# An integer feed-forward with features on the partitions, and a mixture's routing done earlier, on one Trainium2 core

## The reference

```python
probs = jax.nn.softmax(flat @ gate_W.T, axis=-1)
top_v, top_i = jax.lax.top_k(probs, 2)
routed = sum over e of gates[:, e] * (silu(flat @ w1_e[e]) * (flat @ w3_e[e])) @ w2_e[e]
```

```python
def act_qdq(x):                       # 16 bits, one scale for the tensor
    scale = jnp.maximum(jnp.max(jnp.abs(x)) / 32767.0, 1e-12)
    return jnp.clip(jnp.round(x / scale), -32768.0, 32767.0) * scale
x = act_qdq(x)
up = act_qdq(x @ lpbq_dequant(w_up).T)
gate = act_qdq(x @ lpbq_dequant(w_gate).T)
sig = fixed_qdq_u16(jax.nn.sigmoid(gate))
gate = act_qdq(gate * sig)
o = act_qdq(gate * up)
return o @ lpbq_dequant(w_down).T
```

## Time and profile before

| | us |
|---|---|
| median of three runs | 2027.38 |
| the profiled execution, its own time | 2024.79 |
| its span, first to last instruction | 2023.0 |
| mixture up to its loop (first product of the lists at) | 777.0 |
| integer feed-forward, gate (1413.54 to 1469.11) | 55.6 |
| up (1469.11 to 1525.38) | 56.3 |
| second product and its scales (1525.38 to 1561.26) | 35.9 |
| down (1561.26 to 1619.17) | 57.9 |

### The profile page before, as it was taken

One profiled execution on the slowest core, in us unless ns is written; L12 is line 12 of the kernel. 1 busy time (PEld: TensorE's weight loads), 2 busy tenths in 40 slices (PEclk: granted clock), 3 DMA queues, 4 the chain that ended last, 5 costly groups with the idle time before them and its releaser, 6 DMA issues. The chain is left out here.

```text
span 2023.0 us, 38916 instructions
## 1 busy us (share of the span) xinstructions
PE 1860.2 (92%) x13727; PEld 1509.8 (75%) x13728; DVE 1258.4 (62%) x4605; ACT 833.9 (41%) x2271; POOL 278.8 (14%) x514
## 2 busy tenths in 40 slices
PE   8899998999998999999999998997992989999987
PEld 6567766667766998999999998776551867778754
DVE  7768875877786271111111145677788539999988
ACT  3433335565554111111111111775487424445468
POOL 2001112000001051000000044432000320001022
PEclk9999998999999899999999999899995989999999
DMA  6211112111110913222222012110100031111100
GB/s 230 89 55 44 51 47 79 43 70 56 43 43 8 303 55 107 88 86 86 88 86 86 26 53 58 55 44 9 58 1 0 0 107 35 36 38 37 27 11 33
DMA packets 106724, 124.98 MB, mean 62 GB/s; under 512 B 36160, under 2 KB 85832, under 8 KB 104776
## 3 DMA queue, kind: packets, MB, share of 16 engines
q1 hardware_dynamic: 95704, 107.64, 16.1%
q0 software_dynamic: 3072, 8.39, 1.3%
q10 hardware_dynamic: 7792, 6.95, 1.0%
HBM read 86.39 MB, written 36.63 MB: 61 GB/s over the span
## 5 line engine op out<-in xcount | busy, mean ns | idle before, releaser
L1804 DVE TENSOR_TENSOR me_h<-me_sg,me_ps_u 128x512 f32<-128x512 f32 x106 | 72.8, 687 | 273.2 <-PE me_ps_u L1615 273.1
L1756 ACT ACTIVATE me_sg<-me_ps_g 128x512 f32<-128x512 f32 x106 | 63.3, 597 | 363.7 <-PE me_ps_g L1615 363.7
L1276 ACT ACTIVATE ca_e<-ca_scored,ca_neg_max 128x256 f32<-128x256 f32 x256 | 127.2, 499 | 110.4 <-DVE ca_neg_max L1335 110.4
L1615 PE MATMUL me_ps_g<-me_x_turned,me_w 128*128 128x128 f32 x1184 | 145.8, 277 | 1.9 <-issue 1.9
L1615 PEld LDWEIGHTS me_ps_g<-me_x_turned,me_w 128*128 128x128 f32 x1184 | 142.2, 194 | 4.2 <-issue 2.3
L1615 PE MATMUL me_ps_u<-me_x_turned,me_w 128*128 128x128 f32 x1184 | 144.3, 275 | 0.0
L1623 PE MATMUL me_ps_y<-me_w,me_h 128*128 128x256 f32 x592 | 140.0, 380 | 0.0
L1615 PEld LDWEIGHTS me_ps_u<-me_x_turned,me_w 128*128 128x128 f32 x1184 | 138.2, 192 | 0.0
L2995 ACT ACTIVATE sc_y_all<-ss_v 128x16 f32<-128x16 f32 x256 | 60.9, 238 | 148.3 <-DVE ss_v L3060 146.8
L1623 PEld LDWEIGHTS me_ps_y<-me_w,me_h 128*128 128x128 f32 x592 | 106.9, 191 | 11.3
L1335 DVE CUSTOM_DVE_ANT_0 ca_scored<-ca_main,ca_mask_add 128x256 f32<-128x256 f32 x256 | 93.0, 420 | 25.9 <-PE ca_main L1219 25.9
(11 more groups left out here) (465 smaller groups left out, 4374.3 us busy)
## 6 DMA issues: line engine op xcount, KB each, us to landing
me_w<-in_L_ffn_w_e SPq DMA_DIRECT2D x24, 1024.0 KB, 8.1
ca_k_list<-kv_out SPq DMA_DIRECT2D x28, 256.0 KB, 2.3
ca_v_list<-kv_out SPq DMA_DIRECT2D x28, 256.0 KB, 2.3
sk_gb<-scan_g_band SPq DMA_DIRECT2D x14, 512.0 KB, 3.6
moe_x_list<-me_zeros SPq DMA_DIRECT2D x1, 5248.0 KB, 21.2
me_x_tile<-moe_x_list SPq DMA_DIRECT2D x38, 128.0 KB, 2.0
moe_y_list<-me_y ACTq DMA_DIRECT2D x37, 128.0 KB, 1.7
ca_kT<-ca_k_list SPq DMA_DIRECT2D x4, 1024.0 KB, 4.8
```

The costliest lines, as they stand in the source:

```text
L1276: nc.scalar.activation(e[:, g % 3, e_, it, :], scored[:, g % 2, e_, it, :], ACT.Exp, scale=-1.0, bias=neg_max[:, g % 2, n:n + 1], accum_ou ...
L1615: last = nc.tensor.matmul(ps[:, j * P:(j + 1) * P], w[:, n, kt, f:f + P], x[:, kt, :], start=(kt == 0), stop=(kt == KD - 1))
L1756: nc.scalar.activation(sg[:, c, :], ps_g[c][:, :], ACT.Silu).then_inc(done, 1)
L1804: nc.vector.tensor_tensor(h[:, c, :, :].rearrange("p j n -> p (j n)"), sg[:, c, :], ps_u[c][:, :], ALU.mult).then_inc(done[c], 1)
```

## The change

In the integer feed-forward the gate and up products are computed turned: the weights are stationary, 128 features of them, and 1024 tokens are streamed. The result has features on the partitions, in 12 units (6 blocks of features by 2 halves of the tokens) in place of 16 tiles of 768. So the down product can take h as it is, and `turn_h` and `copy_h` go. The elementwise steps work on 1024 columns in place of 768. The ring of integers has three buffers of 1024 in place of four of 768. x is rounded, turned and copied in pairs of tiles. The 16 groups of the next weights are spread over 12 units by `parts_beside`. In the mixture the choice of experts comes before tile 0, the counts inside it, and the placing, cut in two, in tile 1; POOL waits after each three tiles of the scatter until these have landed.

```diff
@@ stage_moe
+    GROUP = 3
+            def count_rows(at):
+                if at != 4:
+                    return
+                pe.wait_ge(both_ready, 1)
+                nc.tensor.matmul(ps_r[:, 0:TILES * E], before[:, :], flat, start=True, stop=True)
...
-                    early(t)
-                if t == 2:
-                    pe.wait_ge(both_ready, 1)
...
+                    early(t, count_rows if t == 0 else nothing)
@@ DVE
             shift_logits()
-            early(0)
             choose_experts()
-            early(1)
+            early(0, behind=scan_counts)
+            early(1, place_experts, place_tokens)
             early(2)
-            scan_counts()
             early(3)
-            place_tokens()
@@ POOL
             for t in range(TILES):
+                if t % GROUP == 0 and t > 0:
+                    pool.wait_ge(scattered, 16 * TOP * t)
@@ int_gate_first, now int_turned
+    WIDE = 1024
+    UNITS = 2 * FT
+    PAIRS = TILES // 2
-    RING = 4
+    RING = 3
-        gi, ui = st.sb("gi", [P, RING, FF], I16), st.sb("ui", [P, RING, FF], I16)
+        gi, ui = st.sb("gi", [P, RING, WIDE], I16), st.sb("ui", [P, RING, WIDE], I16)
+        def piece(w, n):
+            c, f = divmod(n, FT)
+            return w[:, f, WIDE * c:WIDE * (c + 1)]
+        def parts_beside(n):
+            return range(n * len(parts) // UNITS, (n + 1) * len(parts) // UNITS)
@@ PE
+            def half(w, n, side):
+                c, f = divmod(n, FT)
+                t = 8 * c + 4 * side
                 for kt in range(KD):
-                        last = nc.tensor.matmul(ps[t % 2][:, lo:hi], xT[:, t, kt * P:(kt + 1) * P], wT[:, w, kt, lo:hi],
+                    last = nc.tensor.matmul(ps[n % 2][:, side * 512:(side + 1) * 512], wT[:, w, kt, f * P:(f + 1) * P],
+                                            xT[:, t:t + 4, kt * P:(kt + 1) * P], start=(kt == 0), stop=(kt == KD - 1))
-            for t in range(TILES):
-                if t + 1 < TILES:
-                    turn_x(t + 1)
-                gate_product(t)
+            for n in range(2, UNITS):
+                if n + 2 < PAIRS:
+                    turn_x(n + 2)
+                gate_half(n, 0)
+                gate_half(n, 1)
-            for t in range(TILES):
-                up_product(t)
-                turn_next(t)
+            for n in range(UNITS):
+                up_product(n)
+                for g in parts_beside(n):
+                    turn_next(g)
-            schedule(pe, TILES, ((2, turn_h), (3, down)))
+            schedule(pe, TILES, ((2, down),))
@@ ACT
+            for n in range(UNITS - 1):
+                if n + 4 < PAIRS:
+                    copy_x(n + 4)
+                keep_gate(n)
+                if n in (6, 8, 10):
+                    ternary((n - 6) // 2)
-            for t in range(TILES):
-                if t + 1 < TILES:
-                    integers(t + 1)
-                sigmoid(t)
-                keep_up(t)
-                if t >= 1:
-                    copy_next(t - 1)
+            for n in range(UNITS):
+                if n + 1 < UNITS:
+                    integers(n + 1)
+                sigmoid(n)
+                keep_up(n)
+                if n >= 1:
+                    for g in parts_beside(n - 1):
+                        copy_next(g)
-            schedule(act, TILES, ((0, scale_h), (2, copy_h)))
+            schedule(act, TILES, ((0, scale_h),))
```

More of the change, by code:

```diff
@@ L1931, in place_tokens @@
                 link(nc.vector.tensor_copy(table[:, :], first[0:1, :]))
+            def place_tokens():
+                first = starts[:, 4, :]
                 link(nc.vector.tensor_tensor(place[:, 0, :, :], scan[:, 4, :, :], sums[:, :, :], ALU.subtract))
@@ L2443, in gate_product, with turn_x @@
[L2443 to L2451, removed]
-                else:
-                    pe.wait_ge(up_kept, t - 1)
-                multiply(1, t, up_mm)
+            def turn_x(p):
+                pe.wait_ge(x_ready, p + 1)
+                if p >= 2:
+                    pe.wait_ge(xT_ready, p - 1)
+                for m in range(2):
+                    for kt in range(KD):
+                        lo = m * D + kt * P
+                        last = nc.tensor.transpose(ps_x[p % 2][:, lo:lo + P], xi[:, p % 2, m, kt * P:(kt + 1) * P],
+                                                   core.ident[:, :])
+                last.then_inc(x_ps, 1)
@@ L2470, in _ @@
             turn_x(0)
-            for t in range(TILES):
-                if t + 1 < TILES:
-                    turn_x(t + 1)
-                gate_product(t)
-            pe.wait_ge(ident_ready, 1)
-            for t in range(TILES):
-                up_product(t)
-                turn_next(t)
-            pe.wait_ge(product, 2 * TILES - 1)
-            for _ in range(WARM):
[L2481 to L2492, removed]
+            turn_x(1)
+            gate_half(0, 0)
+            turn_x(2)
+            gate_half(1, 0)
+            turn_x(3)
+            gate_half(0, 1)
+            gate_half(1, 1)
+            for n in range(2, UNITS):
[3 more added lines that the diff above has]
+                gate_half(n, 1)
+            pe.wait_ge(ident_ready, 1)
+            for n in range(UNITS):
+                up_product(n)
+                for g in parts_beside(n):
+                    turn_next(g)
+            pe.wait_ge(product, 2 * UNITS - 1)
+            for _ in range(WARM):
+                nc.tensor.matmul(ps_x[1][:, 0:P], core.ident[:, :], core.ident[:, :], start=True, stop=True)
             def down(t, par):
@@ L2573, in _ @@
+            for g in parts_beside(UNITS - 1):
+                copy_next(g)
             act.wait_ge(all_scaled, 1)
-            for t in range(TILES):
-                gate_integers(t)
-                up_integers(t)
+            for n in range(UNITS):
+                gate_integers(n)
+                up_integers(n)
             def scale_h(t, par):
                 if later(t):
-                    act.wait_ge(h_ready, t - 1)
-                nc.scalar.activation(a[:, par, :], gate[:, t, :], ACT.Identity, scale=scal[:, 13:14],
+                    act.wait_ge(hT_ready, t - 1)
+                nc.scalar.activation(a[:, par, :, :], out[:, :, t, :], ACT.Identity, scale=scal[:, 13:14],
```

269 lines of the change are left out of this document (127 added, 142 removed).

## The result

The changed kernel takes 2068.24 us (median of four runs, 2067.25 to 2069.34) where the kernel before takes 2026.47 (median of four): a ratio of 1.0208, 95% interval 1.0193 to 1.0224. It is slower by 42 us. The forecast was 2062.5 with 2042 to 2071.

The account below looks back on a forecast made before the run. PE was taken to bound gate and down, VectorE up and the second product. Mixture -2.5, gate +3.4, up +48.6, second product -0.3, down -12.1 sum to +37.1 on 2024.79: 2061.9, taken as 2062.5 us, range 2042 to 2071.

Parts of the forecast that it names:

- both loops: Up: ring of three delays ScalarE's integers; PE's next-weight group waits for a copy behind the same unit's keep; +48.3 us.
- First product: Up: 13.4 us pass from the last gate unit until VectorE's first product, instead of 10.7.
- Short turns: Up: turns held only by the ring of three buffers take 5.23 us where 4.12 was due.
- The long loop with the clock kept: Up: chain through ScalarE, PE and VectorE where a group needs its own unit's copy; 10.0 us, 11.8 with fallen clock.
- Rival (a): Up: widening wins, neither loop bites, up costs -0.1, total 2013.2 us; turns under 4.9 us make it faster; chance 0.10.
- Rival (b): Up: only the ring bites, copies don't hold PE; up +9.6, total 2023.4 us, no change; chance 0.04.
- Rival (c): Up: both loops bite but TensorE's clock is kept, 6 x 1.8 us less, total 2051; chance 0.14.
- A restart: Up: TensorE's clock falls in each of six long idles, costing 1.7 us more and 0.1 on the small group.
- Gate: Gate part: +3.4 us (0 to +6); PE waits 1.8 at units 2 to 5, 0.9 for the fourth pair.
- Second product: Second product: VectorE's 29.6 us becomes 28.6, fill +0.4, last maximum +0.3, ring of three has slack; -0.3.
- Down: Down part: turnings of h go, -12.1 us; +1.7 if the clock fell in the idle before it.
- Mixture: Mixture: slots ready near 694 instead of 721, scatter done at worst 765; gain 1.7 to 3.3 us, taken 2.5.

Follow-up runs that it names:

- the run with the idle filled: Changed kernel, with unread identity products on TensorE in up ahead of eight next-weight groups' copy waits: 2053.65 us, ratio 1.0146.
- the run with both edits: Changed kernel, in up ScalarE copies next weights ahead of its integers, and the integer ring has four buffers: 2015.65 us, ratio 0.9953.
- the run with copies first: Changed kernel, in up ScalarE copies the previous unit's next-weight groups ahead of integers, sigmoid and kept product: 2022.63 us, ratio 0.9996.
- all repairs together: Changed kernel, up copies ahead of integers, four ring buffers, gate keep ahead of the pair copy, 20 warming products for 14: 2006.46 us, ratio 0.9912.
- the run of the mixture's part alone: Kernel before, with only the change's mixture part (earlier choice, counts and placing, scatter in groups of three tiles): 2020.00 us, ratio 0.9976.
- a ring of four: Changed kernel, gate integers in up get four buffers instead of three, copies left in place: 2034.58 us, ratio 1.0053.
- one group a unit: Changed kernel, next-weight groups spread one to each of the first eleven units, the last five behind the twelfth: 2024.37 us, ratio 1.0002.

## Why the prediction was right, step by step

**Up: right, both loops.** First product: 13.4 forecast, 13.5 measured. Short turns: 5.23 forecast, 5.21 measured. Which turns are long: units 2, 3, 5, 6, 8 and 9, six, as forecast. The long loop with the clock kept: 10.0 forecast, 9.8 in the run with the idle filled. Taken apart on the chip: without the copy wait 52.3 us, without the ring wait 59.5, without either 42.5, against 93.6 with both. Rival (a), that widening wins, is what the run with both edits shows once the two waits are out (2015.65 against the rival's 2013.2); but its own condition, turns under 4.9 us, did not hold in the changed kernel. Rival (b), only the ring bites, is the run with copies first (2022.63 against 2023.4; the terms as written add up to 2023.2). Rival (c), clock kept, is the run with the idle filled (2053.65 against 2051).

**Up: one size too small.** A restart was taken from single restarts in the earlier trace rows as 1.7 + 0.1; the six products behind an idle took 5.71, 6.44, 5.92, 4.96, 5.39 and 6.49, a mean of 2.2 over 3.65, and the filled run gives 2.27 a turn where 1.8 was booked: +2.8 over six. With the clock kept the six turns came out 0.4 shorter than booked (58.9 in the filled run, against 6 x 10.0 - 0.7 = 59.3); the 0.7 for narrower copies is in it, since the last three long turns there are 0.11, 0.33 and 0.32 shorter than the first three. Together 2.4, about this part's miss of 2.3. "Were only the first to pay, the sum would be 8.5 less" counts five restarts at 1.7; at the booked 1.8 it is 9.0.

**Gate: right mechanism, two terms wrong.** Four waits of 1.69 (forecast 1.8) and 0.69 for the fourth pair (0.9). But the 5.1 us of DVE waits in the earlier trace rows were booked as a gain nearly whole. The timeline of before has 1.25 and 0.56 of them ahead of its first gate product, a start that was priced separately (+1.2); only 3.3 could go, 1.2 less than the 4.5 booked. And the slow start was booked as becoming shorter, while it became longer. Before, the first eight records took 4.58 where the next eight took 2.75, 1.8 too much. After, two rows of four records took 3.78 and 2.46 and the four turn records between them 1.06, where 1.88, 1.88 and 0.60 are the times at full clock, 2.9 too much. So the miss of 2.4 us is 1.2 for the waits, 1.1 for the longer slow start and 0.7 for the gain that was booked for it, less 0.6 by which the new waits came out under the forecast.

**Second product: right** (-0.3).

**Down: -10.1 for -12.1.** The "+1.7 if the clock fell" was named and costed at nothing, because idles of 1.1 cost nothing before. In the profiled execution the idle was 1.85 and the clock did fall: the records took 1.68 more than in the runs where it held. With the clock kept the part takes 46.1 (all repairs together), -11.8 for -12.1. No run shows why it fell here, so this term is luck either way: with the same 14 warming products it held in five of seven profiled executions, over idles of up to 2.26.

**Mixture: right**, and at the good end of its range. Slots at 692.5 (forecast 694), no late h, 0.5 for the first listed tile, the last scatter issue at 747.4 (at worst 765), and the clock kept behind the 1.9 us, as in the other two executions with this part of the change. The 1.0 us that the execution was ahead before the mixture's first product is not the change's: that work is the same, and the run of the mixture's part alone has that product at 670.9, as before.

The misses of up, gate and down have one sign, +6.7 us, and most of it is time at half clock that was booked too low. The mixture and the start took 1.8 back, which was not foreseen for the start and is luck. The range held what was left, 5.4 over the sum (with 0.5 behind the block), because its upper bound took in restarts that cost half clock for a whole unit.

## What to carry to other kernels

When work of N pieces is spread anew over M steps, ask of each piece not how many there are in a step but how old the release is that it needs. Here the same 16 groups, the same copies and the same queues cost 40 us when a copy was needed in its own turn and at most 1.2 when it was a turn older. A wait that closes a loop through three in-order queues costs its whole length in every turn, while each engine looks half idle, and two such loops don't add: cutting either one gains most (41 or 34 us here), but the last 10 us come only when both are cut. Before a ring is cut to fit memory, look whether a neighbour's buffers are idle in that part.

## What the runs showed of the hardware that I had not expected

The length of an idle doesn't tell whether TensorE's clock falls to its half level behind it. Nearly equal idles ahead of equal records went both ways: 3.02 us (eight records in 5.35) and 3.05 (3.65) with a ring of four; 2.35 (5.32) and 2.35 again (3.65) with one group a unit; 1.86 (192 records in 43.39) and 1.87 (41.71) ahead of down; 1.90 (16 records in 3.50) and 1.89 (2.05) ahead of the mixture's loop. The granted clock behind the two idles of 2.35 was 0.50 and 1.00.

What the engine did shortly before doesn't settle it either. In the mixture the case that fell had more idle close before it, 1.13 us against 0.52. With a ring of four and with one group a unit it was the other way: the idle that cost was the first one after a long stretch of products with almost none, and the later ones, with another idle of over 2 us some 4 to 9 us before them, cost nothing. What decides was not tried by itself and stays open. Behind the long idles, 4.6 to 6.1 us, the records were slow all six times, and the price varied from 1.3 to 2.8 us at the same work.
